# First cross attention of a two-block decoder: where ACT's exponentials stand among its copies of turned scores

## The reference

```python
q = _qdq(x) @ _qdq(wq).T + bq
kv = cond @ wkv.T + bkv
k, v = jnp.split(kv, 2, axis=-1)
...
attn = jax.nn.softmax(jnp.einsum('bnhd,bmhd->bhnm', q, k) * scale, axis=-1)
o = jnp.einsum('bhnm,bmhd->bnhd', attn, v).reshape(B, N, C)
out = _qdq(o) @ _qdq(wp).T + bp
```

## Time and profile before

| what | value |
|---|---|
| median of three runs | 2743.73 us (2739.06 to 2744.71) |
| profiled execution, its own time | 2742.23 us |
| its span | 2740.1 us |
| PE busy | 2500.0 us (91%) |
| PE weight loads | 2012.5 us (73%) |
| DVE busy | 1666.0 us (61%) |
| ACT busy | 1124.3 us (41%) |
| POOL busy | 929.3 us (34%) |
| first maximum of the stage | 352.12 us from the span's start |
| last step's first maximum | 536.63 us |

### The profile page before, as it was taken

The page is one execution under the profiler, slowest core; times in us unless marked ns, Lnnn a source line. Parts: engine busy times, 40 slices in busy tenths (PEclk is TensorE's granted clock), DMA queues, the critical chain, the costliest instruction groups (busy, mean ns, idle before and its releaser), DMA issues. The chain is left out here.

```text
span 2740.1 us, 48300 instructions
## 1 busy us (share of the span) xinstructions
PE 2500.0 (91%) x14839; PEld 2012.5 (73%) x14840; DVE 1666.0 (61%) x3147; ACT 1124.3 (41%) x2325; POOL 929.3 (34%) x942
## 2 busy tenths in 40 slices
PE   8999778879899999799997998999999998999998
PEld 7888656658688787578875886765666687888887
DVE  4536746669777666667675566865343435656564
ACT  2113266623333324455553233756454421444343
POOL 4213101134333235423333212744333322345554
PEclk9999989989899979899998998999999989999999
DMA  5554132125622045478784432444222132666664
GB/s 190 158 144 104 28 99 71 46 94 167 181 68 57 18 147 191 135 219 233 199 223 105 131 72 99 147 132 125 68 72 72 44 129 84 166 154 158 148 164 71
DMA packets 304544, 336.56 MB, mean 123 GB/s; under 512 B 149231, under 2 KB 220063, under 8 KB 302578
## 3 DMA queue, kind: packets, MB, share of 16 engines
q1 hardware_dynamic: 233170, 256.24, 30.2%
q0 software_dynamic: 20640, 51.74, 9.6%
q10 hardware_dynamic: 50560, 26.34, 3.3%
HBM read 235.70 MB, written 98.56 MB: 122 GB/s over the span
## 5 line engine op out<-in xcount | busy, mean ns | idle before, releaser
L898 PE MATMUL e_psum<-e_up_hi,hT_hi 128*128 x672 | 245.6, 365 | 15.4 <-DVE hT_lo L867 11.3
L900 PE MATMUL e_psum<-e_up_hi,hT_lo 128*128 x672 | 237.3, 353 | 0.0
L899 PE MATMUL e_psum<-e_up_lo,hT_hi 128*128 x672 | 236.7, 352 | 0.0
L1918 POOL TENSOR_TENSOR joint_a_p<-joint_a_p,joint_a_rinv 112x487 f32<-112x487 f32 x128 | 125.3, 999 | 187.0 <-DVE joint_a_rinv L1966 186.5
L1569 POOL TENSOR_TENSOR self_a_p<-self_a_p,self_a_mx 112x448 f32<-112x448 f32 x96 | 96.0, 1000 | 206.0 <-DVE self_a_mx L1626 206.0
L1971 DVE TENSOR_REDUCE joint_a_mx<-joint_psum 112x1 f32<-112x487 f32 x128 | 85.0, 664 | 118.4 <-PE joint_psum L1938 117.8
L898 PEld LDWEIGHTS e_psum<-e_up_hi,hT_hi 128*128 128x128 f32 x672 | 128.1, 191 | 35.1 <-issue 25.2
L794 ACT ACTIVATE e_gate<-e_psum 128x352 f32<-128x352 f32 (+1 forms) x86 | 44.4, 516 | 249.8 <-PE e_psum L900 249.3
L873 DVE TENSOR_TENSOR hT_lo<-e_psum,hT_hi 128x256 fp32r<-128x256 f32 (+2 forms) x138 | 55.7, 435 | 144.7 <-ACT hT_hi L812 144.5
L1660 ACT ACTIVATE self_a_p<-self_a_p 112x448 f32<-112x448 f32 x128 | 71.6, 574 | 167.6 <-POOL self_a_p L1569 114.5
L900 PEld LDWEIGHTS e_psum<-e_up_hi,hT_lo 128*128 128x128 f32 x672 | 127.8, 190 | 11.8
(11 more groups left out here) (565 smaller groups left out, 7348.5 us busy)
## 6 DMA issues: line engine op xcount, KB each, us to landing
e_up_raw<-in_L_ffn_w SPq DMA_DIRECT2D x64, 512.0 KB, 5.3
e_up_raw<-in_L_ffn_w SPq DMA_DIRECT2D x64, 352.0 KB, 4.3
e_dn_raw<-in_L_ffn_w SPq DMA_DIRECT2D x16, 1024.0 KB, 15.6
q_all<-p_p_t_stage ACTq DMA_DIRECT2D x56, 256.0 KB, 2.3
e_dn_raw<-in_L_ffn_w SPq DMA_DIRECT2D x16, 512.0 KB, 6.1
x_first<-q_all SPq DMA_DIRECT2D x32, 224.0 KB, 2.7
v_ctx<-front_c_v_stage SPq DMA_DIRECT2D x24, 250.0 KB
x_others<-k_ctx SPq DMA_DIRECT2D x8, 750.0 KB, 5.1
```

Source lines behind the costliest of these rows:

```text
L898: pe.matmul(out, lhs[0], rhs[0], start=k == 0, stop=False)
L899: pe.matmul(out, lhs[0], rhs[1], start=False, stop=False)
L900: return pe.matmul(out, lhs[1], rhs[0], start=False, stop=k == n_k - 1)
L1918: pool.tensor_tensor(p[:, r, 0:S], p[:, r, 0:S], rinv[:, r:r + 1].to_broadcast([T, S]), ALU.mult).then_inc(p_ready, 1)
```

## The change

ACT's generator of `CrossAttentionPart` alone is rewritten. The loop over a step's exponentials becomes a function of a list of heads, and it is called twice: for heads 0 and 1 at the start of the first half, and for heads 2 and 3 at the start of the second.

```diff
         def scalar(act):
-            yield
-            yield
-            for step in range(n_all + LE):
-                for t in items(step, LT)[0:2]:
-                    copy_turned(act, t)
-                b = closed(step, LP + 1, n_steps)
-                if b is not None:
-                    act.wait_ge(pv_done, (b + 1) * n_groups)
-                    act.copy(by_value[:, :, :], ps[:, o_bank, 0:n_groups * T].rearrange("p (j t) -> p j t", j=n_groups)).then_inc(o_copied, 1)
-                yield
-                for i in items(step):
+            def exponentials(pair):
+                for i in pair:
                     b, h, r = i // n_items, i % n_items, i % RING
                     act.wait_ge(neg_ready, i // 2 + 1)
                     reuse(act, t_done, i - RING + 1)
...
                     act.activation(p[:, r, :], ps[0:T, s_banks[i % N_S], 0:S], ACT.Exp, bias=neg[:, r:r + 1], scale=scale,
                                    accum_out=rsum[:, b % 2, h:h + 1]).then_inc(exp_done, 1)
+
+            yield
+            yield
+            for step in range(n_all + LE):
+                exponentials(items(step)[0:2])
+                for t in items(step, LT)[0:2]:
+                    copy_turned(act, t)
+                b = closed(step, LP + 1, n_steps)
+                if b is not None:
+                    act.wait_ge(pv_done, (b + 1) * n_groups)
+                    act.copy(by_value[:, :, :], ps[:, o_bank, 0:n_groups * T].rearrange("p (j t) -> p j t", j=n_groups)).then_inc(o_copied, 1)
+                yield
+                exponentials(items(step)[2:])
                 for t in items(step, LT)[2:]:
                     copy_turned(act, t)
                 yield
```

More of the change, by code:

```diff
@@ L1810, in scalar @@
         def scalar(act):
+            def exponentials(pair):
+                for i in pair:
+                    b, h, r = i // n_items, i % n_items, i % RING
+                    act.wait_ge(neg_ready, i // 2 + 1)
+                    reuse(act, t_done, i - RING + 1)
+                    if h == 0:
+                        reuse(act, o_evac, b - 1)
+                    act.activation(p[:, r, :], ps[0:T, s_banks[i % N_S], 0:S], ACT.Exp, bias=neg[:, r:r + 1], scale=scale,
+                                   accum_out=rsum[:, b % 2, h:h + 1]).then_inc(exp_done, 1)
             yield
```

## The result

The changed kernel takes 2817.59 us (median of four runs, 2815.69 to 2826.13) against 2741.39 (2739.03 to 2744.71) of the kernel before on the same chip: ratio 1.0283, 95% interval 1.0267 to 1.0299. The way was forecast, the size was not: 76 us and not 52, just above the range's upper end of 2816. The profiled execution took 2817.72 us, its span is 75.5 us longer than the one before.

The account below looks back on a forecast made before the run. Quiet steps were taken as bound by a loop through PE, DVE and ACT, most others by DVE. Terms 4.2 + 39.0 + 0 + 2.5 + 6.6 = 52.3 us on 2742.2 gave 2795; range 2773 to 2816.

Parts of the forecast that it names:

- The loop of a quiet step: Steps 3 to 7, with little output work beside them: cycle from 4.94 to 5.78 us, +4.2 us in all.
- Types 0, 1 and 2: Steps 8 to 30 with number modulo 4 equal to 0, 1, 2: periods of 6.25, 7.80 and 9.43 us.
- ACT's 62 added changes of function: ACT switching more often between exponentials and copies: costed at nothing, bounds 0 and +2 us.
- Type 3: Steps from 8 on with number modulo 4 equal to 3, with `hT_hi`: period of 7.87 us at the full clock.
- Tail, +2.5: From step 31 on: PE's next transposes wait for later copies of heads 2 and 3, 6.6 for 4.07 us, +2.5 us.
- Step 6, +0.84: One of steps 3 to 7, with a read-out besides: same 0.84 us longer, nothing added for the read-out.
- The clock, +6.6, bounds 0 and 15: PE stands 5 us before steps with `hT_hi`, then works at the lower clock: 1.1 us each in six steps.
- start and tail: Steps 0 to 2 taken at 0, bounds -1 and +2.5 us; the end from step 31 on at +2.5 us.
- Rival B: PE's clock falls everywhere in the stage: 2823 us if in half of steps 3 to 30, 2851 in all; 13%.
- over 65 the clock: Sign for the whole stage: longer by over 65 us would prove the clock estimate wrong.
- Rivals A and C: A: exponentials' loop alone pays, 18.9 us, 2761, 12%. C: not slower, first exponential leads, 8.7 us gained, 2733.5, 3%.
- 62 x 2.7: Rejected reading for ACT: a 2.7 us table switch at each added change of function, given as 165 us.

Follow-up runs that it names:

- e5: Changed order only in the six steps with number modulo 4 equal to 2 from step 8 on, otherwise the kernel before: 2761.73 us, ratio 1.0074.
- e8: Kernel before with exponentials split in two pairs, the first pair behind the first two copies and the read-out but ahead of `hT_hi`: 2741.72 us, ratio 1.0004.
- e13: Changed kernel plus unused PE products ahead of the third head's transposes, 9, 7, 0, 12 by step modulo 4 from step 8, 7 in steps 3, 4, 5, 7: 2805.27 us.
- e9: Changed kernel plus unused PE products ahead of the third head's transposes, 5, 5, 0 and 18 by step modulo 4: 2817.21 us, 1.0268 of the kernel before.
- e4: Changed order only in steps 0 to 7, otherwise the kernel before: 2751.96 us, ratio 1.0032.
- e7: Changed order only in steps with number modulo 4 equal to 0 or 1 from step 8 on, otherwise the kernel before: 2775.61 us, ratio 1.0128.
- e11: Kernel before plus 8 unused PE products at the start of steps with number modulo 4 equal to 0: 2737.73 us, ratio 0.9981.
- e2: Kernel before plus 16 unused PE products at the start of steps with number modulo 4 equal to 0: 2748.26 us, ratio 1.0022.
- e1: Changed kernel plus unused PE products ahead of the third head's transposes, 14, 14, 0 and 36 by step modulo 4: 2925.25 us, 1.0681 of the kernel before.
- e3: Kernel before, in its own order, without the three unused small PE products ahead of the transposes in each step: 2756.50 us, ratio 1.0052.

## Why the prediction was wrong

- *The loop of a quiet step, with PE and not the exponentials as what is late next:* right, 5.73 for 5.78.
- *Types 0, 1 and 2:* right at the full clock, 6.26, 7.8 and 9.44 for 6.25, 7.80 and 9.43. e5 shows type 2 alone.
- *ACT's 62 added changes of function, at nothing:* right, by the rows given under e8.
- *Type 3:* 7.87 worked out, 8.03 and 8.13 in the two steps of e13 that had the full clock, and 8.02 in the first of e9; the other four of e9 had it too, but there the fill ran past the copies. Right to 0.3 us.
- *Tail, +2.5:* 2.5 measured, in part by luck. The sixth share of the clock term also fell there, so the sum had 3.6; and the row from which the tail was worked out, PE's next transposes, came at R+7.87 and not at 6.6 (617.52, at the lower level), of which the rest of the stage took up 1.3.
- *Step 6, +0.84:* too small, and not by the clock alone. The value product of a closing step waits for DVE's o to leave the bank. In the trace after (timeline, step 6), PE stands 0.83 us after the read-out's transposes and starts when o is done; the row names no releaser, the wait is in the program (`reuse(pe, o_evac, b)`):

```profile
392.72 0.69 DVE L1798 TENSOR_TENSOR cross_a_o<-cross_psum,cross_a_rinv 112x512 f32<-112x512 f32 x1 [2.11 <-PE cross_psum L1761]
...
393.51 1.35 PE L1774 MATMUL cross_psum<-cross_a_pt,x_others 125*32 125x112 f32 x24 [0.83 <-issue]
...
394.79 1.61 PE L1744 MATMUL cross_psum<-x_others 32*112 32x375 f32 x8
```

The wait was there before (timeline of before, step 6), where the value product came at R+3.52 and the scores did not hang on it:

```profile
388.46 0.78 PE L1774 MATMUL cross_psum<-cross_a_pt,x_others 125*32 125x112 f32 x24 [0.83 <-issue]
```

Now it comes at R+5.23 and all behind it is late. In type 2 DVE's queue hides it, in step 6 nothing does. The 2.11 us missing can be divided by the rows: from value product to scores 1.28 us and from scores to the next R 1.82, against 0.72 and 1.11 in step 3 at the full clock, so 1.27 is the lower level. That leaves 0.84 for the wait, and 7.06 for step 6 at the full clock (an estimate; no run has it).
- *The clock, +6.6, bounds 0 and 15:* this is the step that failed, in its place and in its size. I let PE stand for 5 us between types 2 and 3, took the lower level for what follows in type 3, and left types 0, 1 and the quiet steps at 1.00. In the changed kernel there is no such standing: from step 3 to the last, PE's longest wait is 2.02 us. The fall comes earlier, behind waits of under 2 us, as in steps 10 and 11:

```profile
422.50 0.46 PE L1750 MATMUL cross_psum<-ident 128*128 128x128 f32 x2 [1.97 <-ACT cross_a_pt L1808]
...
425.12 1.35 PE L1774 MATMUL cross_psum<-cross_a_pt,x_others 125*32 125x112 f32 x24 [0.83 <-issue]
...
432.26 0.46 PE L1750 MATMUL cross_psum<-ident 128*128 128x128 f32 x2 [1.87 <-ACT cross_a_pt L1808]
```

The value product of step 10 already runs at half rate (1.35 for 0.78), in the middle of type 2, and what follows it at that rate fills most of the 5 us. The clock also falls within types 0 and 1: step 8 of the changed kernel ran at 1.00 in 6.26, step 9 behind it had 0.82 and took 9.34. Against my terms, steps of type 0 took 11.1 us more in all (8.11 for 6.25, six times), type 1 7.9 (9.12 for 7.80), the quiet steps with step 6 4.8, type 2 0.3, and type 3, with its term, 0.5. That and -1.3 for start and tail are the 23 us between 52.3 and 75.5.

With the full-clock values for types 0 to 3 and the quiet steps, and 7.06 for step 6, the stretch from first to last R would be 229.0 us (17.7 + 4 x 5.73 + 7.06 + 6 x 6.26 + 6 x 7.78 + 6 x 9.44 + 5 x 8.08). So the order's chain is about 44.5 us of the 73 (43.2 forecast), and the clock about 28.6 (5.5 forecast for these steps). The first is shown part by part in e4 to e7 and in the full-clock steps. The second is a difference. That it is the clock is shown for single steps (same instructions, same order, 5.73 at 1.00 and 7.06 at 0.77), and in e13 for the types that came back to their full-clock values; but no kernel held the changed order at the full clock throughout, so the 28.6 is not shown in one piece. The 184.5 of before has dips of its own: type 0 took 5.56 on the mean there and 4.66 in step 28, which ran at 1.00. Between two kernels at the full clock the order would cost more than 44.5.

Rival B had the mechanism, with half of the steps hit, and 2823; I gave it 13% and argued from steps that stood for 0.88 us. The lower level once entered was carried on into the following steps (0.50 in steps 19 and 20 of the changed kernel). My upper bound of 15 had the scores and one step behind, not types 0 and 1 throughout. The forecast's own sign, "over 65 the clock", did point at it: the span grew by 75.5. Rivals A and C found nothing for them. Two slips in the working move nothing: from copy to scores PE needs 2.40 us by the quiet step's own sum, not 2.3, and 62 x 2.7 is 167, not 165.

## What to carry to other kernels

Moving work ahead on an engine that waits anyway looks free, but whoever waits for what is now behind it pays: count from the release of the moved instruction to the next use of each one it was put in front of. Where PE's order is fixed, price each new wait twice, once as the wait and once as all PE work that follows at half the clock until it is seen to rise again, in the steps that follow too. Unused products in a gap can pay, but little here (0.2% for 8 in one gap, e11), and only as many as fit at the lower level: 16 in the same gap cost 0.2% (e2), and 36 in another made type 3 take up to 22.5 us for 9.1 (e1).

## What was not expected of the hardware

- In the order of before PE stood for 0.9 us of 4.94 in each quiet step at 1.00, and for 1.3 of 4.67 in e3. In the changed kernel it stood for 1.80 us in each quiet step: the step at 369.76 ran at 1.00, the next (375.49) fell to 0.77, and the one after it took 5.73 again. With the standing filled (e13) all of them took 5.73. The length of a wait by itself does not tell: in step 22 of e5 PE stood for 2.03 and 0.83 us as in type 2 of the changed kernel, and the value product behind took 0.78 (496.80), where it took 1.35 there. What decides it is left open here.
- The lower level did not end with the step, though no wait of PE there was longer than 2.02 us. Windows of the changed kernel, steps 19 to 21 (types 3, 0 and 1), with PE busy for 8.2 of 8.8 us in the second:

```profile
496.98:506.30 9.32, 6.89 (x51) 4.94 (x50) 5.03 (x12) 4.21 (x13) 1.20 (x1) 0.50 0.34 105
506.30:515.14 8.84, 8.18 (x55) 6.07 (x56) 2.12 (x6) 4.43 (x13) 0.00 (x0) 0.50 0.01 3
515.14:525.11 9.97, 9.28 (x62) 7.21 (x62) 3.82 (x8) 3.89 (x12) 0.00 (x0) 0.62 0.03 2
```

In e3 PE was busy for the whole of a step at 0.50.
- Between exponentials and copies ACT shows no gap and no table load in the changed kernel's stage (the rows given under e8). The Trainium skill (ScalarE: Activation LUTs, "Table sets: the hidden batching unit") says that copies are in every table set, and the trace agrees.
